# Gated cross-attention and top-1 expert layer: context packed on 128 partitions, the issue order of all loads rewritten

## The reference

```python
h = jnp.einsum('eth,efh->etf', x, w1)      # x: layernorm(x), w1 = w2 = ctx_1024
g = jax.nn.gelu(h, approximate=True)
out = jnp.einsum('etf,efh->eth', g, w2)
...
x = x + jnp.tanh(g_xattn[0]) * _L0_xattn_ref(_layernorm(x, axis=-1), ctx_1024, ctx_1024)
x = x + jnp.tanh(g_ffn[0]) * _L0_ffn_ref(_layernorm(x, axis=-1), gate_w, gate_b, w1, b1, w2, b2)
```

## Time and profile before

| | us |
|---|---|
| runs of the kernel: median (lowest to highest, 3 runs) | 135.09 (134.66 to 138.9) |
| the profiled execution: span from first to last instruction | 134.5 |
| median of the runs over that span | 0.6 |
| PE busy in the span | 112.0 (83%) |

### The profile page before, as it was taken

One profiled execution on the slowest core, in us unless ns is written; L12 is line 12 of the kernel. 1 busy time (PEld: TensorE's weight loads), 2 busy tenths in 40 slices (PEclk: granted clock), 3 DMA queues, 4 the chain that ended last, 5 costly groups with the idle time before them and its releaser, 6 DMA issues.

```text
span 134.5 us, 2238 instructions
## 1 busy us (share of the span) xinstructions
PE 112.0 (83%) x742; PEld 101.2 (75%) x743; DVE 53.8 (40%) x210; ACT 28.7 (21%) x82; POOL 32.9 (24%) x70
## 2 busy tenths in 40 slices
PE   5955992996874868999599986999999999999930
PEld 5855881895773747999499966999998989999810
DVE  0505032766447042557489621424232324232210
ACT  4620220321321130243024301313040313111000
POOL 7404021434122001202752247002020202020220
PEclk9996589689999777799999999999999999999999
DMA  4856766375688999574339999999999200000010
GB/s 92 229 145 176 191 178 209 123 204 157 201 214 264 256 313 410 199 241 171 82 96 376 388 383 409 344 421 422 417 392 422 105 4 29 1 5 34 5 41 24
DMA packets 9644, 28.14 MB, mean 209 GB/s; under 512 B 1125, under 2 KB 5919, under 8 KB 7456
## 3 DMA queue, kind: packets, MB, share of 16 engines
q1 hardware_dynamic: 7600, 24.89, 53.0%
q0 software_dynamic: 864, 2.12, 5.4%
q10 hardware_dynamic: 1168, 0.98, 2.5%
HBM read 26.13 MB, written 2.11 MB: 210 GB/s over the span
## 4 chain that ended last, share of the span: by engine, by line
PE 68%; DMA 17%; issue 8%; DVE 2%; SPq 1%; POOL 1%; POOLq 0%; DVEq 0%
PE bank L950 24%; PE bank L959 21%; DMA x<-in_x 8%; PE bank L877 8%; PE bank L864 6%; DMA region<-in_ctx_rows 6%; DMA region<-x_rows,from_row 3%; PE bank L895 2%; PE bank L924 2%; PE bank L886 2%; PE bank L937 1%; POOL out_rows L326 1%; PE bank L854 1%; PE bank L906 1%; SPq L219 1%
## 5 line engine op out<-in xcount | busy, mean ns | idle before, releaser
L950 PE MATMUL bank<-region,w 128*128 128x128 f32 x288 | 35.2, 277 | 1.7 <-issue 1.7
L950 PEld LDWEIGHTS bank<-region,w 128*128 128x128 f32 x288 | 33.8, 192 | 2.6 <-issue 2.1
L959 PE MATMUL bank<-w,region 128*128 128x256 f32 x144 | 32.6, 379 | 0.0
L959 PEld LDWEIGHTS bank<-w,region 128*128 128x128 f32 x144 | 26.7, 190 | 3.3
L437 ACT ACTIVATE region<-bank,smalls 128x128 f32<-128x128 f32 x40 | 12.5, 363 | 42.4 <-PE bank L950 42.4
L864 PE MATMUL bank<-xnT,region 128*125 128x112 f32 x96 | 14.7, 312 | 7.9 <-issue 4.9
L864 PEld LDWEIGHTS bank<-xnT,region 128*125 128x125 f32 x96 | 13.5, 223 | 8.9 <-issue 8.9
L326 POOL DMA_INDIRECT out_rows<-region,to_row x9 | 8.9, 990 | 41.2 <-DVE region L769 40.6
L877 PE MATMUL bank<-region,w 125*112 125x256 f32 x48 | 15.9, 482 | 1.6 <-issue 1.6
L753 DVE TENSOR_SCALAR region<-bank,smalls 128x128 f32<-128x128 f32 x32 | 9.6, 345 | 15.5 <-PE bank L950 14.9
L321 POOL DMA_INDIRECT region<-x_rows,from_row x9 | 9.3, 1029 | 16.8 <-issue 10.8
(11 more groups left out here) (115 smaller groups left out, 92.9 us busy)
## 6 DMA issues: line engine op xcount, KB each, us to landing
w<-in_w1t SPq DMA_DIRECT2D x8, 1024.0 KB
w<-in_w2t SPq DMA_DIRECT2D x8, 1024.0 KB
region<-in_ctx_cols SPq DMA_DIRECT2D x8, 375.0 KB, 6.9
region<-in_ctx_rows SPq DMA_DIRECT2D x8, 375.0 KB
b2b<-in_b SPq DMA_DIRECT2D x1, 1024.0 KB, 18.3
x_rows<-x ACTq DMA_DIRECT2D x8, 113.8 KB, 5.3
x<-in_x SPq DMA_DIRECT2D x1, 448.0 KB, 11.3
x<-in_x SPq DMA_DIRECT2D x2, 112.0 KB, 2.3
```

The lines of the kernel that those rows point to most:

```text
L950: mm = pe.matmul(hT_ps[k][:, part % 2 * P:(part % 2 + 1) * P], w1[:, e, n * H + part * P:n * H + (part + 1) * P], xgT[:, j % 2, n * P:(n + ...
L959: mm = pe.matmul(y[:, 0:D], hidT[:, q, part, :], w2[:, e, part * D:(part + 1) * D], start=(part == 0), stop=(part == KH - 1))
```

## The change

The host packs, for each batch, the transposed context (750 numbers a partition) and the three row groups of the context (768 numbers a partition, padded from 125 to 128 partitions with zeros) into one array `ctx` of 128 partitions by 1518 numbers. A context is now one load of 759 KB, except context 0, which comes as two loads with x of batch 1 between them. All of x is issued before context 1. The waits are: contexts 1 and 2 are issued, then a wait for context 1; contexts 3 and 4, then a wait for context 3; contexts 5 to 7, then a wait for context 7. After that SP issues the weights of expert 0, b2, and the weights of experts 1 to 5 without any wait between them. Experts 6 and 7 wait only for the tiles that lie in their place. Every load of a context or a weight has its own semaphore. The arithmetic and PE's order are as before; only the layout of `region` differs.

```diff
@@ tiles @@
+CW = KD * CTX + CC * D
-        region = sb("region", [P, B * (KD * CTX + CC * D)])
-        cxT = region[:, 0:B * KD * CTX].rearrange("p (b n) -> p b n", b=B)
-        cx = region[:, B * KD * CTX:].rearrange("p (b n) -> p b n", b=B)
+        region = sb("region", [P, B * CW])
+        cxs = region[:, :].rearrange("p (b n) -> p b n", b=B)
+        cxT, cx = cxs[:, :, 0:KD * CTX], cxs[:, :, KD * CTX:CW]
...
@@ SP @@
-            def load_context(b, q):
-                sp.dma_start(cxT[:, b, :], ctx_cols[b]).then_inc(cxT_in[q], 16)
-                sp.dma_start(cx[0:CR, b, :].rearrange("p (c d) -> p c d", c=CC),
-                             ctx_rows[b].rearrange("(c p) d -> p c d", p=CR)).then_inc(cx_in[q], 16)
+            def load_context(b):
+                sp.dma_start(cxs[:, b, :], ctx[b]).then_inc(cx_in[b], 16)
...
             load_x(0, 1).then_inc(x_in[0], 16)
+            sp.dma_start(cxT[:, 0, :], ctx[0, :, 0:KD * CTX]).then_inc(cxT0_in, 16)
             load_x(1, 1).then_inc(x_in[1], 16)
-            load_context(0, 0)
+            sp.dma_start(cx[:, 0, :], ctx[0, :, KD * CTX:CW]).then_inc(cx_in[0], 16)
             load_x(2, 2).then_inc(x_in[2], 16)
-            load_context(1, 1)
-            sp.wait_ge(cxT_in[0], 16)
-            sp.wait_ge(cx_in[0], 16)
-            load_context(2, 0)
             load_x(4, 4).then_inc(x_in[3], 16)
-            sp.wait_ge(cxT_in[1], 16)
-            sp.wait_ge(cx_in[1], 16)
-            load_context(3, 1)
-            with sp.Fori(2, B // 2) as t:
-                for q in range(2):
-                    sp.wait_ge(cxT_in[q], 16 * t)
-                    sp.wait_ge(cx_in[q], 16 * t)
-                    load_context(2 * t + q, q)
-
-            load_expert(0, 0)
+
+            for e in range(2):
+                load_context(2 * e + 1)
+                load_context(2 * e + 2)
+                sp.wait_ge(cx_in[2 * e + 1], 16)
+            load_context(5)
+            load_context(6)
+            load_context(7)
+            sp.wait_ge(cx_in[7], 16)
+
+            load_expert(0)
             sp.dma_start(b2b[:], b2.partition_broadcast(P)).then_inc(b2_in, 16)
-            sp.dma_start(w1[:, 1, :], w1t[1]).then_inc(w1_in[1], 16)
-
-            sp.wait_ge(xn2T_ok, B)
-            sp.wait_ge(w1_in[0], 16)
-            sp.dma_start(w1[:, 2, :], w1t[2]).then_inc(w1_in[0], 16)
-            for q in range(2):
-                sp.wait_ge(first_in[q], 16)
-            sp.wait_ge(xg_in[0], 16)
+            for e in range(1, E - 2):
+                load_expert(e)
+
+            sp.wait_ge(xnT_done, B)
             sp.wait_ge(xgT_done, 1)
             sp.wait_ge(xn2T_done, B)
-            sp.dma_start(w2[:, 1, :], w2t[1]).then_inc(w2_in[1], 16)
...
-            with sp.Fori(2, E // 2) as t:
-                for q in range(2):
-                    sp.wait_ge(w1_in[q], 16 * t)
-                    sp.wait_ge(w2_in[q], 16 * t)
-                    load_expert(2 * t + q, q)
+            for e in range(E - 2, E):
+                load_expert(e)
@@ PE, scores and attend @@
-                pe.wait_ge(cxT_in[b % 2], 16 * (b // 2 + 1))
+                pe.wait_ge(cx_in[b] if b else cxT0_in, 16)
...
-                pe.wait_ge(cx_in[b % 2], 16 * (b // 2 + 1))
+                if b == 0:
+                    pe.wait_ge(cx_in[b], 16)
@@ PE, up and down @@
-                pe.wait_ge(w1_in[e % 2], 16 * (e // 2 + 1))
+                pe.wait_ge(w1_in[e], 16)
...
-                pe.wait_ge(w2_in[e % 2], 16 * (e // 2 + 1))
+                pe.wait_ge(w2_in[e], 16)
```

More of the change, by code:

```diff
@@ L47, with gated_cross_attention_moe @@
 NOWHERE = 65536.0
-def gated_cross_attention_moe(nc, x, ctx_rows, ctx_cols, small, w1t, w2t, b2, out):
+def gated_cross_attention_moe(nc, x, ctx, small, w1t, w2t, b2, out):
     x2_dram = nc.dram_tensor("x2_rows", (TOKENS, ROW), F32, kind="Internal").ap()
@@ L163, in gated_cross_attention_moe @@
         small_in, b2_in = sem("small_in"), sem("b2_in")
[L164 to L167, removed]
+        cxT0_in = sem("cxT0_in")
+        cx_in = [sem(f"cx_in{b}") for b in range(B)]
+        w1_in = [sem(f"w1_in{e}") for e in range(E)]
+        w2_in = [sem(f"w2_in{e}") for e in range(E)]
         pool_step = sem("pool_step")
@@ L208, in _, with load_expert @@
         def _(sp):
-            def load_context(b, q):
-                sp.dma_start(cxT[:, b, :], ctx_cols[b]).then_inc(cxT_in[q], 16)
-                sp.dma_start(cx[0:CR, b, :].rearrange("p (c d) -> p c d", c=CC),
-                             ctx_rows[b].rearrange("(c p) d -> p c d", p=CR)).then_inc(cx_in[q], 16)
-            def load_expert(e, q):
-                sp.dma_start(w1[:, e, :], w1t[e]).then_inc(w1_in[q], 16)
-                sp.dma_start(w2[:, e, :], w2t[e]).then_inc(w2_in[q], 16)
+            def load_context(b):
+                sp.dma_start(cxs[:, b, :], ctx[b]).then_inc(cx_in[b], 16)
+            def load_expert(e):
+                sp.dma_start(w1[:, e, :], w1t[e]).then_inc(w1_in[e], 16)
+                sp.dma_start(w2[:, e, :], w2t[e]).then_inc(w2_in[e], 16)
             def load_x(b, n):
@@ L250, in _ @@
+            load_expert(0)
+            sp.dma_start(b2b[:], b2.partition_broadcast(P)).then_inc(b2_in, 16)
+            for e in range(1, E - 2):
+                load_expert(e)
+            sp.wait_ge(xnT_done, B)
             sp.wait_ge(xgT_done, 1)
             sp.wait_ge(xn2T_done, B)
-            sp.dma_start(w2[:, 1, :], w2t[1]).then_inc(w2_in[1], 16)
-            sp.wait_ge(w2_in[0], 16)
-            sp.dma_start(w2[:, 2, :], w2t[2]).then_inc(w2_in[0], 16)
-            sp.wait_ge(w1_in[1], 16)
@@ L256, in _ @@
-            sp.dma_start(w1[:, 3, :], w1t[3]).then_inc(w1_in[1], 16)
-            sp.wait_ge(w2_in[1], 16)
-            sp.dma_start(w2[:, 3, :], w2t[3]).then_inc(w2_in[1], 16)
-            with sp.Fori(2, E // 2) as t:
-                for q in range(2):
-                    sp.wait_ge(w1_in[q], 16 * t)
-                    sp.wait_ge(w2_in[q], 16 * t)
-                    load_expert(2 * t + q, q)
+            for e in range(E - 2, E):
+                load_expert(e)
         @block.gpsimd
@@ L1074, in _ @@
                 turn_block(BLOCKS, 1)
-            pe.wait_ge(w2_in[1], 16 * E // 2)
+            pe.wait_ge(w2_in[E - 1], 16)
             pe.wait_ge(o_ok, E - 1)
@@ L1121 @@
         "x": np.ascontiguousarray(x).reshape(TOKENS, D),
-        "ctx_rows": np.ascontiguousarray(ctx_1024),
-        "ctx_cols": np.ascontiguousarray(
-            np.asarray(ctx_1024).transpose(0, 2, 1).reshape(B, KD, P, CTX).transpose(0, 2, 1, 3)).reshape(B, P, KD * CTX),
+        "ctx": np.ascontiguousarray(np.concatenate([
+            np.asarray(ctx_1024).transpose(0, 2, 1).reshape(B, KD, P, CTX).transpose(0, 2, 1, 3).reshape(B, P, KD * CTX),
+            np.pad(np.asarray(ctx_1024).reshape(B, CC, CR, D).transpose(0, 2, 1, 3).reshape(B, CR, CC * D),
+                   ((0, 0), (0, P - CR), (0, 0)))], axis=2)),
         "small": np.ascontiguousarray(np.concatenate([
```

## The result

The changed kernel takes 127.12 us (median of 4 runs, 126.17 to 127.42) against 135.56 for the kernel before (134.66 to 138.9, the runs shown above and one more): a ratio of 0.937, 95% interval 0.929 to 0.945. Forecast were 125.2 us and a range of 118 to 131. The profiled execution has a span of 124.4 us; the sum of the prediction gave 124.6. The 0.6 compared the span of one execution with the median of others. Executions of one kernel differ here by 0.5 to 5.6 us, and every ratio with an interval uses only those within 1.5% of their kernel's fastest.

The account below looks back on a forecast made before the run. The prediction took slow context loads to bound stage one and PE the rest: 134.5 - 13.0 - 5.1 + 1.5 + 3.1 + 2.8 + 2.5 - 1.7 = 124.6 us of span, plus 0.6 gives 125.2 us, range 118 to 131.

Parts of the forecast that it names:

- What bounds the kernel: Up to 53 us, context loads, `cx` on about a third of the DMA engines; after 67.19 us, PE.
- Step 1: The start: context 1 lands between 8.5 and 10.2 us, so `scores(1)` starts at 10.0 instead of 11.62.
- Step 2: Contexts 2 to 7: no `scores` waits for context 7; `scores(7)` at 31.3 instead of 44.30, gain 13.0 us (10.7 to 14.6).
- Step 3: Tail of stage one: wait ahead of `attend(7)` and half clock go, 5.1 us won (4 to 5.1).
- Step 4: The price: freely queued weights share the DMA engines; store +1.5, first gather +3.1, block 3 +2.8, clock +2.5, weight wait -1.7 us.
- The third term: Gathers beside weights land 3.8 us apart, so block 3 comes 2.8 us later (0 to 5).
- the term for the half clock: PE idles before `turn_block(1)` and block 3; one or two clock dips cost 2.5 us (0 to 4).
- starving gathers: Rival: POOL's nine gathers beside queued weights make it slower than before, 139.8 us at spacing 8.3 us; chance 0.04.
- the cheap collision: Rival: stores and gathers lose only about 2 us beside weights; 117.3 us, 116 to 120.5; chance 0.22.
- attention bound otherwise: Rival: DVE's order or half clock holds attention iterations at 4.6 us, `scores(7)` at 37; 131 us; chance 0.12.
- the slow context: Rival: packed contexts still take some 4.6 us each, context 7 lands at 38; 131 to 132 us; chance 0.05.
- long turns between the gathers: Rival: each gather waits for a whole weight load's rows, 5.5 us apart instead of 3.8; 130.3 us; chance 0.06.

Follow-up runs that it names:

- rows125: The changed kernel with each context loaded in two parts out of the packed array, `cx` on 125 partitions of 3072 bytes; 133.51 us.
- rows128: The changed kernel with each context loaded in two parts out of the packed array, `cx` on 128 partitions of 3072 bytes; 125.12 us.
- pack_only: The kernel before with only the packed context, weights held back and two contexts under way as before; 119.47 us.
- order_only: The changed kernel with all of the new order, but contexts as two loads as before, `cx` on 125 partitions; 136.2 us.
- x_late: The changed kernel with the 448 KB of x of batches 4 to 7 issued behind context 1 instead of ahead; 124.11 us.
- hold_all: The changed kernel with that x load behind context 1 and weights behind w1 of expert 1 held until the first three gathers landed; 122.34 us.
- g_gather: The changed kernel with the weights of experts 2 to 7 issued only when the first three gathers have landed; 122.06 us.
- shallow: The changed kernel with each expert's weights from the third on issued only when those two before have landed; 125.97 us.
- g_store: The changed kernel with the weights of experts 2 to 7 issued only when the eight stores have landed; 125.0 us.

## Why the prediction was right, and where its terms were off

**What bounds the kernel.** Right, and shown: `cx` on a third of the engines (`rows125` against `rows128`). The prediction took the slow `cx` to be what the change removes; `pack_only` and `order_only` show that the packing alone does it.

**Step 1** failed in size. Context 1 landed at 12.20, outside the 8.5 to 10.2 given. The first 8 us of flow ran at 277 GB/s, below the lower bound of 315, though the DMA share was 1.02: the engines were busy, and slower than the prediction allowed. And context 2, issued 0.5 us behind context 1, flowed beside it. In the window 2.00 to 12.20 some 3.1 MB moved, not 2.5:

```profile
2.00:10.00 8.00, 7.28 (x35) 6.43 (x33) 3.14 (x10) 3.21 (x8) 3.79 (x18) 1.00 1.02 277
10.00:12.20 2.20, 0.00 (x0) 0.00 (x0) 0.83 (x2) 0.38 (x1) 0.75 (x2) 1.00 0.99 397
```

**Step 2** was nearly right. Of the five iterations from `scores(2)` to `scores(7)` three are 3.35 to 3.36 us as read from the earlier trace rows, the others 3.12 and 3.89, 17.1 in all against 16.8; the step from `scores(1)` to `scores(2)` took 4.68, inside 2.9 to 5.6. But PE's gap ahead of context 1 was again followed by half clock: `scores` took 2.33 and `attend` 1.97 us against 1.31 and 1.30. From `scores(1)` to `scores(7)` it is 21.8 us, where the prediction had taken 21.3 from a range of 19.7 to 23.6. So of the 2.8 us by which `scores(7)` came late (34.10 instead of 31.3), 2.3 are step 1's and 0.5 are this step's. The 10.2 us won lie just outside the 10.7 to 14.6.

**Step 3** was right: 5.0 against 5.1 us. `first_block` took 1.34 us, close to the 1.5 of the prediction.

**Step 4** had the place right and two sizes off. The gather: 3.1 expected, 3.14 measured. The store: I counted 7 us to landing, it took 8.65, so 2.6 us instead of 1.5. The third term, 2.8 us for block 3, did not exist. It took the spacing of 3.8 us from gathers that POOL had issued one by one behind waits. The first four gathers start 1.3 to 1.6 us apart, the fourth lands at 62.3, and DVE takes it up at 65.72 without waiting:

```profile
54.60 1.00 POOL L303 DMA_INDIRECT region<-x_rows,from_row  x1 [0.30 <-issue]
```

Block 1 to block 3 took 1.4 us longer, and the chain has it in the slow first instructions: 0.69, 1.71 and 2.98 us for L920, L942 and L933, against 0.44, 0.86 and 2.68 before. That is the term for the half clock, put at 2.5.

**So the sum was right to 0.2 us by luck.** Its errors cancel: 2.8 too much won at the start, 2.8 too much charged for the gathers; the rest, store +1.1 and clock -1.1, did the same. That the collision would cost some 7 us was foreseen, how it splits only in part. The time of 127.1 us lies 1.9 above the 125.2, because what surrounds the span is 1.8 and not 0.6 us, and because the profiled execution was the fastest of the four.

Two figures of the working are off without harm to the forecast. The highest sum of all terms is 134.7 us of span, or 135.3 with the 0.6, not 134. And by the rival's own formula starving gathers would set the end from a spacing of 6.4 us on; 7.6 is where the kernel becomes slower than before.

The rivals: the cheap collision is excluded by 8.65 and 6.83 us; attention bound otherwise by the 3.36; the slow context by the landings, from 12.20 to 27.85 us for six more contexts, 2.6 us each; long turns between the gathers and starving gathers by PE, which waits for no later gather.

What the prediction didn't see is that the change is two changes of opposite sign. It priced the collision but never asked what the packing would do with the old order. `pack_only` answers: 119.5. The order costs 7.6 us of what the packing gives. The two profiled executions, 124.4 and 118.4 us, show where their 6.0 us lie. Up to `scores(7)` the changed kernel is 3.2 us behind, of which moving the x load behind context 1 gives back 2.6 (`x_late`). Then it loses 2.6 to the store, 3.1 to the gather and 1.4 up to block 3, and wins back 4.3 behind block 3, where `pack_only` waits 2.32 us for weights and takes 5.44 us for the `up` behind that wait instead of 3.57. So letting the weights go early is worth something too. No run has both that gain and free transfers: `hold_all` traded the collision for waits of its own.

## What to carry to other kernels

When a load is slow, look at the DMA share while it flows alone. Here it was 0.32, the shape of the load was the limit, and padding 125 partitions to 128 won more than any order did. A transfer that the next stage waits for, however small, should find no bulk load in flight: here 114 KB took 8.65 us instead of 2.1 to 2.5. A queue of at most two experts' loads instead of some ten loads did not help, only their absence did, and even that only as far as the loads held back are not needed soon. When a change has two parts, price each without the other.

## What the runs showed of the hardware that was not expected

- A store of 114 KB issued beside weights at 415 to 426 GB/s lands after 8.35 to 9.3 us (eight executions), one with free engines after 2.1 to 2.5. The first gather, 128 rows, lands after 6.2 to 7.2 us beside weights and after 3.46 to 3.75 without.
- SP's issue of a load is not always 0.4 us. In the changed kernel the thirteenth load from the first weights on, with some ten not yet landed, took 7.08 us to issue, and the next four 1.7 to 2.4 each. A load of 1 MB takes 2.5 us at 420 GB/s, so the issues probably follow the landings.
- Two context loads of 759 KB issued 0.5 us apart flow side by side: the first landed 8.6 us after its issue and the second 9.9 us after its own.
- Kernels that are the same up to 27 us ran the second `scores` in 1.53 us (`g_gather`, `shallow`) or in 2.33 and 2.83 (the changed kernel, `g_store`); the longer times stood behind the longer gaps of PE.
